# A recurrent attention layer and a routed feed-forward layer on one core: GpSimd's row sends split around the normalisation, the first tile table in two halves, weights cast sooner, the last two tiles exchanged, the gate folded into the output sums

## What is computed

```python
# layer 1: chunked linear recurrence over the normalised input, 4 heads of 64
n = _layernorm(x)
v = (n @ W_write.T)                       # values
inter = einsum('bij,bcj->bci', W, rk_c) * g_p
S = einsum('bcd,bkd->bck', rk_c, wk_c)
intra = einsum('bck,bkd->bcd', S * M, v_c)
W_new = g_C * W + einsum('bci,bcj->bij', v_c * g_w, wk_c)
x = x + (n + (alpha * reads) @ W_read.T)
# layer 2: 8 experts, the best 2 for each token
probs = softmax(_layernorm(x) @ gate_w.T); topk_probs, topk_idx = top_k(probs, 2)
h = gelu(w1[e] @ m + b1[e]); y = w2[e] @ h + b2[e]     # for e in topk_idx
x = x + sum(y * topk_probs)
```

## Time and profile before

| | |
|---|---|
| device time, median of 3 runs | 581.01 us (576.79 to 581.92) |
| the profiled execution | 580.57 us, of it the span 578.8 us |
| PE busy, share of the span | 536.8 us, 93% |
| DVE | 444.0 us, 77% |
| ACT | 333.6 us, 58% |
| POOL | 244.1 us, 42% |

### The profile page before, as it was taken

The page is one execution under the profiler, slowest core; times in us unless marked ns, Lnnn a source line. Parts: engine busy times, 40 slices in busy tenths (PEclk is TensorE's granted clock), DMA queues, the critical chain, the costliest instruction groups (busy, mean ns, idle before and its releaser), DMA issues. The chain is left out here.

```text
span 578.8 us, 17513 instructions
## 1 busy us (share of the span) xinstructions
PE 536.8 (93%) x5246; PEld 422.6 (73%) x5246; DVE 444.0 (77%) x1314; ACT 333.6 (58%) x827; POOL 244.1 (42%) x305
## 2 busy tenths in 40 slices
PE   8779799999989998999999999999999999999990
PEld 7567587878768765777777777777777777777760
DVE  6889699999866999677768777777776867777760
ACT  6799688989824834445454545445545545555530
POOL 3143878888854743333223323233333233323223
PEclk8899799999969999999999999999999999999996
DMA  5655668786442542543444334444443444333432
GB/s 166 242 171 180 213 227 262 234 261 220 148 117 80 133 85 42 81 71 67 69 68 69 65 60 65 73 76 75 76 75 66 72 67 69 64 62 62 69 46 27
DMA packets 85143, 63.32 MB, mean 109 GB/s; under 512 B 54208, under 2 KB 77376, under 8 KB 85056
## 3 DMA queue, kind: packets, MB, share of 16 engines
q1 hardware_dynamic: 71472, 44.21, 29.6%
q0 software_dynamic: 13296, 18.00, 17.0%
q10 hardware_dynamic: 288, 0.00, 0.0%
HBM read 37.56 MB, written 24.62 MB: 107 GB/s over the span
## 5 line engine op out<-in xcount | busy, mean ns | idle before, releaser
L1488 PE MATMUL psum<-arena,weights 128*128 128x256 f16 (+1 forms) x2208 | 278.4, 248 | 2.8 <-ACT arena L727 2.3
L1488 PEld LDWEIGHTS psum<-arena,weights 128*128 x2208 | 187.5, 98 | 79.8 <-issue 3.8
L524 POOL DMA_INDIRECT out<-arena,tile_in x71 | 112.8, 1589 | 252.2 <-ACT arena L735 162.7
L1503 PE MATMUL psum<-weights,arena 128*128 x568 | 214.6, 379 | 1.4 <-DVE arena L1120 1.4
L727 ACT ACTIVATE arena<-psum,b_cur 128x256 f32<-128x256 f32 (+1 forms) x368 | 132.0, 424 | 138.4 <-PE psum L1488 130.5
L1505 PE MATMUL psum<-weights,arena 128*128 x568 | 154.8, 273 | 0.0
L1120 DVE TENSOR_TENSOR arena<-arena 128x512 f16<-128x512 f32 x142 | 98.3, 692 | 4.9
L1118 DVE CAST arena<-arena 128x512 f16<-128x512 f32 x142 | 64.2, 452 | 34.3 <-ACT arena L727 33.4
L502 POOL DMA_INDIRECT sent_rows<-arena,tiny x64 | 65.8, 1028 | 25.0 <-issue 20.1
L1503 PEld LDWEIGHTS psum<-weights,arena 128*128 128x128 f16 x568 | 55.6, 98 | 7.8 <-issue 2.0
L1505 PEld LDWEIGHTS psum<-weights,arena 128*128 128x128 f16 x568 | 55.6, 98 | 4.5
(11 more groups left out here) (164 smaller groups left out, 631.6 us busy)
## 6 DMA issues: line engine op xcount, KB each, us to landing
weights<-in_experts SPq DMA_DIRECT2D x32, 512.0 KB, 5.3
arena<-sent_rows SPq DMA_DIRECT2D x100, 64.0 KB
arena<-in_b SPq DMA_DIRECT2D x46, 128.0 KB, 3.1
arena<-in_x SPq DMA_DIRECT2D x16, 256.0 KB, 3.6
out<-arena SPq DMA_DIRECT2D x16, 256.0 KB, 6.4
arena<-sent_rows SPq DMA_DIRECT2D x84, 32.0 KB
sent_rows<-pad SPq DMA_DIRECT2D x8, 265.0 KB, 6.5
tile_in<-sent_rows SPq DMA_DIRECT2D x71, 4.5 KB, 2.4
```

The lines of the kernel that those rows point to most:

```text
L524: pool.indirect_dma_start(out=out, out_offset=bass.IndirectOffsetOnAxis(ap=at_u, axis=0), in_=yout[:, u % 4], in_offset=None, compute_op=A ...
L1488: last = pe.matmul(ps_h[:, f % 2, mm * n:(mm + 1) * n], w1_of(e_of[i], k, lo, per * (f - GROUP[i]) + mm), turned[:, i % 2, part, k, 0:n], ...
L1503: pe.matmul(to, h_hi[:, z % 4, at], w2_of(e_of[t], m), start=(m == 0), stop=(m == MF - 1), skip_group_check=True)
```

## The change

It has six parts.

1. **POOL's step** (`norm`, `mark`, `send`): the four sends of a chunk go one step later, as two and two around the first normalisation, and marking the tokens stands behind them, ahead of the second normalisation. In the steps from 16 on a chunk's sends follow at once.
2. **Weight pieces**: SP starts the loads of pieces 0 to 3 at the program's head, ahead of the third chunk of x; ACT casts pieces 0 and 1 before `chunk_values(0)`, and in steps 3 and 4 one piece earlier and (step 3) one later in its order.
3. **`early`** becomes `early_count` at the head of DVE's step 16 and `early_table` at its end.
4. **The last two tiles** exchange their widths: tile 44 is a half one, tile 45 a wide one; the tables get two copies more each.
5. **The gate**: `prepare` also writes the gate times 1/64 (`gate_scaled`); ACT's `gated_bias` writes bias times gate into the output unit one group before the tile's end, where `scale` stood one group later; `finish` adds the two PSUM halves times the scaled gate to it.
6. POOL's adds wait for `finish` (`ybias_done`) and no longer for ACT.

```diff
-WIDE = [i < NE or i % 2 == 0 for i in range(NT)]
+WIDE = [i < NE or i == NT - 1 or (i % 2 == 0 and i != NT - 2) for i in range(NT)]
...
+            for j in range(4):
+                load_piece(j)
+
             def step(n):
 
                 par = n % 2
                 if active(n + 1, 0) and n > 0:
                     load_x(n + 1, 1 - par)
                 for j in splits(n + 1):
-                    load_piece(j)
+                    if j > 3:
+                        load_piece(j)
...
+            def send(m, b):
+
+                for name in ("token_done", "xm_done", "gates_done", "slot_i_done"):
+                    reached(pool, name, m)
+                for k in range(2):
+                    at_bk = slot_i[:, m % ROWS, 2 * b + k:2 * b + k + 1]
+                    pool.indirect_dma_start(
+                        out=sent, out_offset=bass.IndirectOffsetOnAxis(ap=at_bk, axis=0),
+                        in_=row[:, m % ROWS, b, :], in_offset=None).then_inc(row_out[m % ROWS], 16)
+
...
+                if LAG < n <= NCH:
+                    send(n - LAG - 1, 0)
                 if active(n, 0):
...
+                    norm_chunk(n)
+                if LAG < n <= NCH:
+                    send(n - LAG - 1, 1)
+                if active(n, LAG):
+                    mark(n - LAG)
+                if active(n, 3):
+                    norm_residual(n - 3)
+                if n >= NCH:
+                    send(n - LAG, 0)
+                    send(n - LAG, 1)
```

ACT's and DVE's step, and stage two:

```diff
+                for j in splits(n)[1:-1][0:1]:
+                    split_high(j)
                 if active(n, 2):
                     chunk_values(n - 2)
                 if active(n, 4):
                     normed_transposed(n - 4)
-                for j in splits(n)[1:]:
+                for j in splits(n)[1:][-1:] if len(splits(n)) < 4 else splits(n)[2:3]:
                     split_high(j)
...
+                for j in splits(n)[3:]:
+                    split_high(j)
...
             chunk_keys(0)
+            split_high(0)
+            split_high(1)
             chunk_values(0)
             chunk_normalise(2)
             chunk_keys(1)
-            for j in splits(2):
-                split_high(j)
+            split_high(2)
...
+            def gated_bias(i):
+
+                came(a, "prep_done", i)
+                a.wait_ge(b2_in[i % 2], 16 * (i // 2 + 1))
+                added_unit(a, UNIT[i + 1] - 5)
                 for u in units(i):
-                    came(a, "ybias_done", u)
-                    a.activation(yout[:, u % 4], yout[:, u % 4], ACT.Copy,
+                    a.activation(yout[:, u % 4], b2_cur[:, i % 2], ACT.Copy,
                                  scale=gate_cur[:, u % 8:u % 8 + 1]).then_inc(S2["yout_done"], 1)
...
-                if g - 3 == GROUP[i + 1] - 1:
-                    scale(i)
+                if g - 3 == GROUP[i + 1] - 2:
+                    gated_bias(i)
...
+                if n == NCH:
+                    early_count()
...
-                if n == NCH:
-                    early()
...
+                if n == NCH:
+                    early_table()
...
+                last.then_inc(S2["gate_done"], 1)
+                came(v, "gate_done", i)
+                for u in units(i):
+                    last = v.tensor_scalar(gate_scaled[:, u % 8:u % 8 + 1], gate_cur[:, u % 8:u % 8 + 1], 1.0 / WSCALE,
+                                           None, ALU.mult)
                 last.then_inc(S2["prep_done"], 1)
...
             def finish(i):
+
+                came(v, "yout_done", UNIT[i + 1] - 1)
                 came(v, "l2_done", GROUP[i + 1] - 1)
-                v.wait_ge(b2_in[i % 2], 16 * (i // 2 + 1))
-                added_unit(v, UNIT[i + 1] - 5)
                 for u in units(i):
-                    v.scalar_tensor_tensor(out=yout[:, u % 4], in0=ps_y[u % 4][:, 1], scalar=1.0 / WSCALE,
-                                           in1=b2_cur[:, i % 2], op0=ALU.mult,
+                    v.scalar_tensor_tensor(out=yout[:, u % 4], in0=ps_y[u % 4][:, 1],
+                                           scalar=gate_scaled[:, u % 8:u % 8 + 1], in1=yout[:, u % 4], op0=ALU.mult,
                                            op1=ALU.add).then_inc(S2["ylow_done"], 1)
                 for u in units(i):
                     came(v, "ylow_done", u)
-                    v.scalar_tensor_tensor(out=yout[:, u % 4], in0=ps_y[u % 4][:, 0], scalar=1.0 / WSCALE,
-                                           in1=yout[:, u % 4], op0=ALU.mult,
+                    v.scalar_tensor_tensor(out=yout[:, u % 4], in0=ps_y[u % 4][:, 0],
+                                           scalar=gate_scaled[:, u % 8:u % 8 + 1], in1=yout[:, u % 4], op0=ALU.mult,
                                            op1=ALU.add).then_inc(S2["ybias_done"], 1)
```

More of the change, by code:

```diff
@@ L162, in build @@
         gate_cur = sb("gate_cur", [P, 8])
+        gate_scaled = sb("gate_scaled", [P, 8])
         tileT = sb("tileT", [P, KD * TILE])
@@ L982, in count_tiles, with early_count @@
                 link(v.tensor_reduce(ends, c4, AX.X, ALU.add))
-            def early():
+            def early_count():
                 reached(v, "base_done", NCH - LAG - 1)
@@ L990, in early, with early_table @@
                 count_tiles(spare, "step", TOK // TILE)
+            def early_table():
                 t = slice(0, NE)
```

74 lines of the change are left out of this document (33 added, 41 removed).

## The result

The changed kernel takes 587.67 us (median of 4 runs, 585.1 to 590.09) where the kernel before takes 580.25: a ratio of 1.0131, 95% interval 1.0097 to 1.0165. It is slower, and the time lies above the top of the forecast's range (587.0). On a second occasion it took 584.86 us beside 580.26, ratio 1.0085 (1.0058 to 1.0111).

What follows compares the result with a forecast made beforehand. PE is busy from 240 to 563 us, so gains lie in stage one, the way into stage two and the tail; POOL's second L491 sets stage one's step. Terms summed to -0.3, so 580.3 us; range 571 to 587.

Steps and rivals of the forecast that it cites:

- start: Start of the pipeline: DVE waits less for the first cast pieces; -0.6 us, between -2.0 and +0.9.
- steps 6 to 8: Stage one: one later send held, +0.6, and step 8 falling to DVE's 9.27 us, -0.4; +0.2 us together.
- steps 9 to 15: Stage one: a held send makes each step 10.80 us instead of 9.72; +7.6 us, bounds -3.2 and +7.6.
- steps 16 and 17: The table no longer stands between L885 and L837, and clock loss is partly regained; -5.7 us, bounds -1.6 and -8.6.
- start of stage two: DVE's added work in prepare and the table copies is nearly all exposed; +1.3 us, ends 0 and +2.
- tail: The last tile's add no longer waits for the adds of the wide tile before; -3.1 us.
- hold A: Stage one: DVE's L767 from 1.93 to 3.15 us after L885, holding POOL instructions that start inside it.
- hold B: Stage one: DVE's L767 from 5.89 to 7.11 us after L885, holding POOL instructions that start inside it.
- The send passes A: Rival, stage one: the send starting 0.02 us ahead of hold A isn't held; steps of 9.72, 574.7 us; chance 0.28.
- sends are not what holds it: Rival, stage one: the holds fall elsewhere and DVE sets all steps at 9.27 us; 571 us; chance 0.12.
- The clock falls in the longer steps: Rival, stage one: PE's hole of nearly 2 us in each 10.80 us step lowers its clock; 588 us; chance 0.14.
- the held case: The forecast's own case, stage one: a send held by hold A, steps of 10.80 us; chance 0.38.

Runs made afterwards that it cites:

- e16: The changed kernel with GpSimd's old order put back and the first split_low of a step moved behind residual_moments: ratio 0.9895 to the kernel before.

## Why the prediction was wrong

Its parts against the traces, in us; "alone" is the run with that part only, against the first trace of the kernel before:

| term | forecast | first trace | again | alone |
|---|---|---|---|---|
| start, to 56.37 | -0.6 | +0.2 | -2.4 | -0.6 |
| steps 6 to 8, to 90.54 | +0.2 | +2.6 | | |
| steps 9 to 15, to 158.58 | +7.6 | +9.4 | | |
| these two together | +7.8 | +12.1 | +12.3 | +11.6 |
| steps 16 and 17 | -5.7 | -2.4 | -4.9 | -5.8 |
| start of stage two | +1.3 | +2.0 | +1.4 | +1.3 |
| tail | -3.1 | -2.6 | -2.4 | -2.6 |
| sum, the difference of the spans | -0.3 | +9.2 | +4.1 | |

**The mechanism was right, and the price of the new order in steps 6 to 15 was too low: +7.8 against +12.1 us, and +12.3 and +11.6 in two other pairs. This is the term that failed.** Steps 9 to 15 were forecast at 10.80 us and take 11.07 on average, 11.12 when settled; steps 6 to 8 at +0.2 and they took +2.6. In the first pair the steps 16 and 17 also brought 3.3 us less than forecast. On the second occasion these brought only 0.8 less and the start 1.8 more than forecast, and 584.86 us would have lain inside the range with the same term just as wrong: the range would have been met by luck.

*The 10.80.* The forecast took 0.17 us from the end of the second product to the send behind it. The earlier trace rows shows 117.14 to 117.49, which is 0.35, with the gain in between; 0.17 was only the bracket. And it was a short gap, behind an instruction just held. Without a hold the same trace has the product of 66.82 end at 67.02 and the send start 0.61 later:

```profile
67.63 1.08 POOL L502 DMA_INDIRECT sent_rows<-arena,tiny  x1 [0.43 <-issue]
```

In the new order the send comes 0.62 behind L479. Against the 0.17 that is 0.45 more, and another 0.05 stands between the last send and the next normalisation, so this starts not at -0.02 but at +0.49 from `chunk_low`. It is then the gain (at 2.05) that stands inside hold A (from 1.93), and the pair of sends ends 0.37 later than forecast. The second normalisation starts at 6.05, inside hold B (from 5.90), where the forecast had it at 5.68, ahead of B, and only its second instruction held. Whichever is held ends with B. So one more instruction is left to do behind B, and the last product ends at 8.55 and not 8.24: these are the 0.3 us.

The step from 137.64 shows the forecast's own case. Its first normalisation starts at 0.00, its second at 5.66, L475 is the instruction held by B, and the step takes 10.83 where 10.80 was forecast. It comes about behind a step in which the clock fell (0.85 granted from 126.68 to 137.64) and GpSimd waited 1.33 us for DVE's numbers of the rows to send (L858); then the steps settle at 11.12 again.

The question on which the forecast put 0.28, whether a send 0.02 ahead of A passes, didn't come up. Even in that step the send starts 2.21 behind `chunk_low`, 0.27 inside A, since the gap behind the gain was 0.42 and not 0.17. A distance that decides by 0.02 us can't be read from rows that were each measured with another neighbour.

*Steps 6 to 8.* The forecast said that step 8 "falls to DVE's 9.27". It took 10.82, as the step from 137.64 does: the new order is in force from the first step that sends from both sides, and there is no step of DVE's between. That is 1.5 of the 2.4 missed. Step 6 takes 0.6 more than before, as forecast, with two sends held (1.82 us each, at 58.72 and 62.81). The other 0.9 is in step 7, which takes 12.18 us and not 11.23, and goes with the clock: PE is busy for all but 0.2 us of that step in both kernels, with the granted clock at 0.79 and 0.86. As an estimate from these, 0.21 of 12.18 us less 0.14 of 11.23 is 1.0 us.

**Steps 16 and 17** were forecast at -5.7, and the part alone brings -5.8. How much it brings goes with the clock. From `chunk_low` of step 16 to the second gelu the traces have, with the mean granted clock of the stretch:

| | us | clock |
|---|---|---|
| table in one, kernel before | 28.4 | 0.82 |
| table in one, new order alone | 26.1 | 0.93 |
| in halves, changed kernel, first trace | 26.0 | 0.87 |
| in halves, changed kernel, again | 23.6 | 0.93 |
| in halves, all parts but the new order | 23.6 | 0.93 |
| in halves, alone | 22.6 | 1.00 |

At the same clock (0.93) the halves are worth 2.5 us, and the rest of the 5.8 came back with the clock, about as the forecast had split it (3.4 and 2.3). The new order alone already brings 2.3 by the clock, so that in the changed kernel less is left to gain. In its first trace the clock fell there:

```profile
170.00:175.00 5.00, 5.00 (x22) 4.06 (x23) 3.17 (x11) 1.86 (x7) 3.29 (x5) 0.66 0.34 125
```

and DVE waited 0.60 and 1.66 us for PE in step 16. What makes the clock fall in one execution and not in another I can't say from these runs.

**Start** came out as forecast where part 2 stands alone (55.78). Over the chips of the first kind `chunk_low` of step 6 has a mean of 56.6 in the six traces without part 2 (55.78 to 57.46) and of 55.8 in the four with it (55.08 to 56.54): a single start varies by more than the term's size. The late third chunk of x is there, 1.12 us. **Start of stage two**: the gate alone adds 1.3 us between the second gelu and the last matmul (378.02 against 376.74), the number forecast; two traces without the gate part have up to 1.0 more there too (377.71 with the table in halves), so this is not exact. In the first trace it was 2.0, with the fall of the clock after 230 us. **Tail**: 12.5 us from the last matmul to the end, against 15.1; in the run with the order exchanged alone 12.5 too, so folding the gate adds nothing to that here.

**The rivals.** "The send passes A", "sends are not what holds it" and their times are refuted by the steps at 115.57 and 137.64. "The clock falls in the longer steps" gives 588 us and the result is 587.67, but by another way: the steps of 11.12 us run at clock 1.00 in the windows from 80 to 120 and from 140 to 160, and at 0.91 once between, for one step. That step (126.68) has no instruction of GpSimd held and takes 10.96 us, less than its neighbours. So the time agrees and the mechanism does not. The range's top went by this rival's price less a little, and left no room for the held case itself coming out 4 us longer. The bounds of the term for steps 9 to 15 were -3.2 and +7.6, with the forecast itself as the upper one: all the ends considered shortened the step.

## What to carry to other kernels

Where GpSimd sets a pipeline's step, its instructions' own times don't tell what an order costs: each one that starts inside a VectorE operation that holds it pays that operation's rest, and a reordering decides by tenths of a microsecond which ones do. Lay the whole cycle out, gaps included, measured from one fixed instruction, before judging an order; and take the distance between two starts from rows in which the same two instructions follow each other, not the bracket alone. When a change has six parts, time them apart: five of these were worth 6 us together, and the sixth cost more than that.

## What the hardware showed that I had not expected

- The first send of a group starts 0.61 to 0.62 us behind the end of the last product, whether a gain of 0.22 us stands between them (the gap is then some 0.43) or nothing does. Behind a hold the gap is 0.17 as a rule: behind the gain that was itself held (1.19 us), and in the kernel before behind a gain of 0.22 that follows the held product. Why the gap is short behind a hold is open.
- A tensor_scalar with one input (1024 float32 to float16, strided) holds GpSimd for its 0.69 us. A memset of the same region, 0.48 us, does not: a power that starts 0.09 into it takes its 0.72.
- An instruction of GpSimd that starts 0.04 us ahead of a hold passes (117.46 against 117.50), one that starts 0.01 into it pays it in full (85.00 against 84.99 in e16, 1.77 us for a power of 0.72).
- The kernel before takes 580 us on three of the five chips of the experiments and 591 and 593 on two. On those two PE's 24 weight loads for the scores take up to 1.14 us in kernels of the old order where they take 0.81 on the others, for instance

```profile
123.76 1.10 PEld L1384 LDWEIGHTS psum<-arena 64*128 64x128 f16 x24 [0.21 <-issue]
```

  (a step of the kernel without the new order, ratio 0.9883), and the step is 10.0 to 10.7 us and not 9.72. Why is open.
